# Gate and up products of two token tiles by Strassen's seven block products, in a PE-filled fp4 feed-forward kernel

## The reference

```python
def fp4_linear(x, w):                       # both sides quantized and dequantized in blocks of 16
    return jnp.einsum('bsk,nk->bsn', fp4_quant_dequant(x), fp4_quant_dequant(w))
x = x + tanh(g_xattn) * attention(ctx, ctx, layernorm(x))          # 512 wide, 77 keys a batch
gate = fp4_linear(layernorm(x), w_gate)     # 4096 x 512 by 512 x 1408
y    = fp4_linear(layernorm(x), w_up)       # the same shape
x = x + tanh(g_ffn) * fp4_linear(silu(gate) * y, w_down)           # 4096 x 1408 by 1408 x 512
```

## Time and profile before

| | us |
|---|---|
| time, median of 3 runs (lowest, highest) | 833.9 (832.92, 834.39) |
| span of the profiled execution, first to last instruction | 832.3 |
| TensorE matmul busy in it | 822.4 |
| VectorE busy | 650.7 |
| ScalarE busy | 459.9 |
| GpSimd busy | 400.5 |
| granted TensorE clock, mean | 1.000 |

### The profile page before, as it was taken

How to read it: one execution, slowest core, us unless ns; L and a number is a source line. 1 busy time by engine, 2 the same in 40 slices (tenths; PEclk the granted TensorE clock), 3 DMA queues, 4 the chain that set the end, 5 groups by cost and what they waited for, 6 DMA issues and landing times.

```text
span 832.3 us, 11653 instructions
## 1 busy us (share of the span) xinstructions
PE 822.4 (99%) x4102; PEld 417.0 (50%) x4102; DVE 650.7 (78%) x967; ACT 459.9 (55%) x930; POOL 400.5 (48%) x333
## 2 busy tenths in 40 slices
PE   9999999999999999999999999999999999999998
PEld 5555445444554445444544454445544454444445
DVE  5887899898998698877878688778876878776654
ACT  2778675547555666456563755366646565344320
POOL 3498797764334353444333543454444533444421
PEclk9999999999999999999999999999999999999999
DMA  9723703553243434532641255224433443222232
GB/s 318 285 70 103 157 13 97 122 128 92 48 80 106 108 82 89 129 56 54 114 120 40 55 110 136 61 60 99 97 61 61 85 85 73 58 54 55 48 75 73
DMA packets 192817, 78.21 MB, mean 94 GB/s; under 512 B 176387, under 2 KB 178037, under 8 KB 192759
## 3 DMA queue, kind: packets, MB, share of 16 engines
q1 hardware_dynamic: 192759, 77.47, 39.6%
HBM read 22.76 MB, written 8.39 MB: 37 GB/s over the span
## 4 chain that ended last, share of the span: by engine, by line
PE 93%; ACT 3%; DVE 2%; issue 1%; DMA 1%; POOL 1%; POOLq 0%; ACTq 0%; DVEq 0%
PE banks L1918 60%; PE banks L2037 27%; DVE banks L1417 1%; PE banks L2053 1%; PE banks L1912 1%; PE banks L1971 1%; PE banks L1999 1%; PE banks L1998 1%; PE banks L2143 1%; DMA x_T<-x_parts 1%; PE banks L2150 0%; PE banks L2008 0%; PE banks L2160 0%; PE banks L2165 0%; PE banks L2155 0%
## 5 line engine op out<-in xcount | busy, mean ns | idle before, releaser
L1918 PE MATMUL banks<-wgu_hi,x_T 128*128 128x512 f16 (+1 forms) x1536 | 439.3, 361 | 1.6 <-DMA x_T<-x_parts 0.9
L1918 PE MATMUL banks<-wgu_lo,x_T 128*128 128x512 f16 (+1 forms) x768 | 277.5, 361 | 0.0
L1918 PEld LDWEIGHTS banks<-wgu_hi,x_T 128*128 128x128 f16 x1536 | 150.3, 98 | 155.6 <-issue 1.3
L2037 PE MATMUL banks<-wd,arena 128*128 128x512 f16 x1023 | 227.2, 379 | 0.0
L2037 PEld LDWEIGHTS banks<-wd,arena 128*128 128x128 f16 x1023 | 99.7, 98 | 117.4 <-issue 0.6
L648 POOL TENSOR_TENSOR arena<-arena,h_r 128x1024 f32<-128x1024 f32 (+1 forms) x60 | 93.2, 1554 | 115.3 <-DVE h_r L1372 115.3
L648 POOL TENSOR_TENSOR arena<-arena,h_s 128x1024 f32<-128x1024 f32 x64 | 90.7, 1418 | 88.6 <-DVE arena L1419 53.6
L1918 PEld LDWEIGHTS banks<-wgu_lo,x_T 128*128 128x128 f16 x768 | 75.1, 98 | 76.8 <-issue 0.3
L648 POOL TENSOR_TENSOR xwork<-xwork,x_s 128x512 f32<-128x512 f32 x32 | 38.4, 1201 | 152.0 <-DVE xwork L1419 152.0
L1052 ACT ACTIVATE arena<-banks,scal 128x512 f32<-128x512 f32 (+1 forms) x96 | 61.9, 647 | 84.9 <-PE banks L1918 84.8
L1571 DVE SCALAR_TENSOR_TENSOR arena<-arena,scal,banks 128x512 f32<-128x512 f32 (+1 forms) x90 | 62.2, 694 | 56.3 <-PE banks L1918 53.5
(11 more groups left out here) (199 smaller groups left out, 1043.6 us busy)
## 6 DMA issues: line engine op xcount, KB each, us to landing
ring<-in_x_dram SPq DMA_DIRECT2D x8, 1024.0 KB, 5.1
out_dram<-ring SPq DMA_DIRECT2D x31, 256.0 KB, 2.2
arena<-in_L_ffn_w_down_dram SPq DMA_DIRECT2D x4, 704.0 KB, 5.0
arena<-in_L_ffn_w_gate_dram SPq DMA_DIRECT2D x5, 512.0 KB, 9.7
arena<-in_L_ffn_w_up_dram SPq DMA_DIRECT2D x5, 512.0 KB, 9.6
ring<-in_L_xattn_Wk_dram SPq DMA_DIRECT2D x4, 256.0 KB, 6.1
ring<-in_L_xattn_Wq_dram SPq DMA_DIRECT2D x4, 256.0 KB, 6.8
wd<-in_ctx_dram SPq DMA_DIRECT2D x1, 1024.0 KB
```

The source lines that it names most:

```text
L1918: ended = e.matmul(at, l, r, start=(i == 0), stop=(i == len(terms) - 1))
L2037: ended = e.matmul(by_k(down_ps(t)[:, :], KD), l, r, start=(k == 0 and i == 0), stop=(k == KH - 1 and i == 2))
```

## The change

Tiles 8 to 29 are taken in 11 pairs (a, a + 1). For chunk 0 alone, the gate and up products of both tiles are one 2 by 2 block product: the rows are the two tiles, the inner blocks the two halves of the 512 inputs, the columns the gate and the up weights. Where the kernel before does eight block products (each two k slices, three matmuls each, 512 columns), the new one does seven, in Winograd's form of Strassen's scheme: `pair_product(a, name)` for P1, P5, P6, P2, P7, P3, P4 in this order. The left-hand sums are made from the quantized x on GpSimd (`sum_x`), cast by ScalarE (`sum_high`), their rest by GpSimd (`sum_low`) and transposed by a DMA through `x_parts` (`sum_turn`): two more passes through that buffer a pair. The four sums of weights T1 to T4, 128 x 1024 each, are made once, amid tiles 4 to 7: on GpSimd three instructions for T3 and T1 and two for T2 and T4 (`sum_weights`) and one each for the rest (`low_weights`), on ScalarE a cast each (`high_weights`). Partial results are passed between banks: `copy_p1` and `copy_u3` copy a bank to a bank, `copy_p5` a bank to SBUF, `add_v` and `add_c22` add on VectorE, and `pair_silu`, `pair_hidden` take the place of silu and the multiply for chunk 0.

For these tiles the hidden parts are 512 columns (chunk 0, the last one ready) and 896 columns (chunks 1 and 2), each with a transpose of its own (`part_turn`), and the down product begins with the groups of chunks 1 and 2. Odd tiles use buffers of their own for the parts and scales. x has a ring of 3 slots, the fourth holds weight sums. All five engines have a new order from the first instruction to the last, written out for tiles 0 to 7 and 28 to 31, and as a loop over four tiles (two pairs) between them.

Of the pieces below, `sum_turn` is SP's, `sum_x` and `sum_low` GpSimd's, the copies ScalarE's, the adds VectorE's; after TensorE's loop the last two pieces are VectorE's and ScalarE's lists for the second pair of the loop.

```diff
-    SLOTS = 4
+    SLOTS = 3
+    FIRST_PAIR, PAST_PAIRS = 8, 30
+        STEPS_OF_PAIR = ("P1", "P5", "P6", "P2", "P7", "P3", "P4")
+        BANK_A, BANK_B, BANK_C, BANK_D, BANK_F = 1, 0, 2, 5, 3
+        SUM_ORDER = ("T3", "T2", "T4", "T1")
...
+            def sum_turn(a, i):
+                w.wait_ge(x_lo, place_of_sum(a, i) + 1)
+                if a > FIRST_PAIR:
+                    w.wait_ge(pair_mm, pair_step(a - 2, "P3" if i else "P7"))
...
+                e.dma_start_transpose(sum_T[i], x_parts[:, :]).then_inc(x_turned, 16)
...
+            def sum_x(a):
+                w.wait_ge(x_lo, place_of_x(a + 1) + 1)
+                near, far = slice(0, D // 2), slice(D // 2, D)
+                e.tensor_tensor(x_q2[:, far], x_q2[:, near], x_q2[:, far], ALU.add).then_inc(*step())
+                e.tensor_tensor(x_q2[:, near], x_q[:, near], x_q2[:, near], ALU.subtract).then_inc(x_summed, 1)
...
+                e.tensor_tensor(x_q[:, near], x_q2[:, far], x_q[:, near], ALU.subtract).then_inc(*step())
...
+                e.tensor_tensor(x_q[:, far], x_q[:, far], x_q[:, near], ALU.subtract).then_inc(x_summed, 1)
+            def sum_low(a, i):
+                e.tensor_tensor(x_parts[:, D:2 * D], (x_q2, x_q)[i], x_parts[:, 0:D], ALU.subtract).then_inc(x_lo, 1)
+            def copy_p1(a):
+                w.wait_ge(pair_mm, pair_step(a, "P1"))
+                w.wait_ge(silu_done, SILU(a + 1, 1))
+                e.copy(bank[BANK_B][:, :], bank[BANK_A][:, :]).then_inc(pair_copied, 1)
+            def copy_p5(a):
...
+                e.copy(p5_sb, bank[BANK_F][:, :]).then_inc(pair_copied, 1)
+            def copy_u3(a):
+                w.wait_ge(pair_mm, pair_step(a, "P7"))
...
+                e.copy(bank[BANK_D][:, :], bank[BANK_B][:, :]).then_inc(pair_copied, 1)
...
+            def add_v(a):
+                w.wait_ge(pair_mm, pair_step(a, "P6"))
+                w.wait_ge(h_made, SILU(a + 1, 1))
+                w.wait_ge(*copied(a, "P5"))
+                e.tensor_tensor(bank[BANK_C][:, :], bank[BANK_B][:, :], p5_sb, ALU.add).then_inc(pair_added, 1)
+            def add_c22(a):
...
+                e.tensor_tensor(h_of(b)[:, 0:BANK], bank[BANK_B][:, :], p5_sb, ALU.add).then_inc(pair_added, 1)
...
+            def pair_product(a, name):
+                tokens, ks, weights, at, opens = {
+                    "P1": (of_a, near, quads["B11"], BANK_A, True),
+                    "P2": (of_a, far, quads["B21"], BANK_A, False),
+                    "P3": (of_v[1], far, quads["B22"], BANK_C, False),
+                    "P4": (of_b, far, sums["T4"], BANK_D, False),
+                    "P5": (of_v[0], far, sums["T1"], BANK_F, True),
+                    "P6": (of_v[1], near, sums["T2"], BANK_B, False),
+                    "P7": (of_v[0], near, sums["T3"], BANK_B, False)}[name]
...
+                elif name == "P6":
+                    frees[BANK_B] = added(a, "C22")
+                    w.wait_ge(*copied(a, "P1"))
+                    w.wait_ge(x_turned, 16 * (place_of_sum(a, 1) + 1))
+                elif name == "P7":
+                    w.wait_ge(*added(a, "V"))
+                elif name == "P4":
+                    frees[BANK_D] = (silu_done, SILU(a + 1, 0))
+                    w.wait_ge(*copied(a, "U3"))
...
+                for k in range(2):
+                    for i, (l, r) in enumerate([(hi[:, k, :], weights[0][:, :, k, :]), (hi[:, k, :], weights[1][:, :, k, :]), (lo[:, k, :], weights[0][:, :, k, :])]):
+                        ended = e.matmul(by_k(bank[at][:, :], 4), l, r, start=(opens and k == 0 and i == 0), stop=(k == 1 and i == 2), skip_group_check=True)
...
-            for t in range(7, NT):
+            for t in range(FIRST_PAIR, PAST_PAIRS - 2, TILES):
+                n = t // TILES + 1
+                gate_up(t, 1, 0)
+                gate_up(t, 2, 0)
+                gate_up(t, 1, 1)
+                gate_up(t, 2, 1)
+                down(t - 2, 0)
...
+                gate_up(t + 3, 1, 0)
+                gate_up(t + 3, 2, 0)
+                gate_up(t + 3, 1, 1)
+                pair_product(t + 2, "P1")
+                gate_up(t + 3, 2, 1)
+                down(t + 1, 0)
+                pair_product(t + 2, "P5")
+                pair_product(t + 2, "P6")
+                pair_product(t + 2, "P2")
+                pair_product(t + 2, "P7")
+                att_values(n, 3)
+                pair_product(t + 2, "P3")
+                down(t + 1, 1)
+                pair_product(t + 2, "P4")
+                down(t + 1, 2)
...
+                hidden(t + 3, 2)
+                h_scales(t + 3, 1)
+                h_low(t + 2, 1)
+                x_low(t + 4)
+                add_v(t + 2)
+                h_round(t + 3, 1)
+                values(n, 3)
+                pair_hidden(t + 2, 0)
+                h_scales(t + 2, 0)
+                add_c22(t + 2)
...
+                gate_silu(t + 3, 2)
+                x_squares(t + 4)
+                sum_high(t + 2, 1)
+                if n + 1 < NBATCH:
+                    ln1_sums(n + 1)
+                h_high(t + 2, 1)
+                copy_p1(t + 2)
+                x_high(t + 4)
+                copy_p5(t + 2)
+                h_squares(t + 3, 1)
+                pair_silu(t + 2, 0)
+                if n + 1 < NBATCH:
+                    ln1_squares(n + 1)
+                copy_u3(t + 2)
```

More of the change, by code:

```diff
@@ L208, in build, with x_whole @@
         xT = [[x_T[i][:, p * KD:(p + 1) * KD, :] for p in range(2)] for i in range(2)]
+        sum_T = [valo[:, i, :].bitcast(F16).rearrange("p (k n) -> p k n", k=2 * KD) for i in range(2)]
+        def x_whole(t):
+            return x_q2 if t >= FIRST_PAIR and t % 2 else x_q
         x_parts = sb("x_parts", [P, 2 * D], F16)
@@ L610, in sync_program @@
             x_turn(5)
+            store(0)
             h_turn(3)
@@ new lines, in pool_program @@
+            h_divide(26, 0)
+            h_divide(27, 0)
+            h_times(26, 0)
+            x_times(29)
+            x_stats(30)
+            sum_x(28)
+            h_divide(28, 1)
+            sum_low(28, 0)
+            h_times(27, 0)
+            sum_low(28, 1)
+            x_times(30)
+            h_times(28, 1)
+            x_stats(31)
+            h_divide(29, 1)
+            h_times(29, 1)
+            h_divide(28, 0)
+            h_divide(29, 0)
+            h_times(28, 0)
+            h_times(29, 0)
@@ L835, in scalar_program @@
+            x_times(31)
+            h_divide(30, 0)
+            h_divide(30, 1)
+            h_times(30, 0)
+            h_times(30, 1)
+            h_divide(31, 0)
+            h_divide(31, 1)
+            h_times(31, 0)
+            h_times(31, 1)
         @block.scalar
@@ L1888, in vector_program @@
-            h_round(NT - 1, 1)
-            finish(NT - 3)
-            h_low(NT - 1, 0)
-            h_low(NT - 1, 1)
-            finish(NT - 2)
+            x_divide(8)
+            hidden(7, 0)
+            hidden(7, 1)
+            x_round(8)
+            h_scales(7, 0)
+            x_low(8)
+            key_low(1)
+            finish(4)
+            key_low(2)
+            h_low(6, 1)
+            hidden(7, 2)
+            h_low(6, 0)
+            h_scales(7, 1)
+            h_round(7, 0)
@@ new lines, in vector_program @@
+            h_round(26, 0)
+            finish(25)
+            h_round(27, 0)
+            x_scales(29)
+            x_divide(29)
+            h_low(26, 0)
+            x_round(29)
+            x_low(29)
+            hidden(28, 1)
+            hidden(28, 2)
+            h_scales(28, 1)
+            h_round(28, 1)
+            x_scales(30)
+            hidden(29, 1)
+            finish(26)
+            x_divide(30)
+            hidden(29, 2)
+            x_round(30)
+            h_low(27, 0)
+            h_scales(29, 1)
@@ new lines, in vector_program @@
+            add_v(28)
+            h_low(28, 1)
+            x_low(30)
+            h_round(29, 1)
+            pair_hidden(28, 0)
+            add_c22(28)
+            h_scales(28, 0)
+            finish(27)
+            pair_hidden(28, 1)
+            h_scales(29, 0)
+            h_round(28, 0)
+            h_round(29, 0)
+            x_scales(31)
+            h_low(28, 0)
+            x_divide(31)
+            x_round(31)
+            hidden(30, 0)
+            x_low(31)
+            hidden(30, 1)
@@ new lines, in vector_program @@
+            h_scales(30, 0)
+            hidden(30, 2)
+            h_scales(30, 1)
+            h_round(30, 0)
+            h_low(29, 1)
+            h_low(29, 0)
+            finish(28)
+            h_round(30, 1)
+            hidden(31, 0)
+            hidden(31, 1)
+            h_scales(31, 0)
+            h_low(30, 0)
+            hidden(31, 2)
+            h_scales(31, 1)
+            h_round(31, 0)
+            h_low(30, 1)
+            h_round(31, 1)
+            finish(29)
+            h_low(31, 0)
@@ new lines, in tensor_program @@
+            gate_up(28, 1, 1)
+            down(26, 1)
```

(31 more changed lines are left out.)

1527 lines of the change are left out of this document (912 added, 615 removed).

## The result

The changed kernel takes 853.36 us (median of 4 runs, 851.88 to 854.21), beside 833.41 for the kernel before on the same chip (832.34 to 834.39): ratio 1.0237, interval 1.0221 to 1.0253. It is slower by 20 us, where 12 us less were forecast. The profiled execution has a span of 852.4 us, and the forecast's span was 819.8: 32.6 us are to be found.

A forecast was written before the change was run, and what follows sets the result against it. TensorE, without gaps in the loop, was taken as the bound: 832.3 - 14.2 + 1.0 + 1.2 + 0.5 - 1.0 = 819.8 us of span, median 1.6 above, 821.4. The likeliest case's range was 818 to 824.5, the overall range 816.5 to 829.

The forecast's parts named there:

- 66 matmuls at 0.216: -14.2.: TensorE, chunk 0 of gate and up: six fewer matmuls a pair in 11 pairs, at 0.216 us each: -14.2 us.
- I take +0.5: Ahead of tile 8: fourteen GpSimd instructions for weight sums, 32 us, may hold VectorE: +0.5 us, bounds 0 and 8.
- The new order ... -1.0: Ahead of tile 8: value_product(4) fills places where TensorE had waited 0.7 and 0.9 us: -1.0 us, bounds -4 and +4.
- The first half of h ... slack 1.4; I take 0.: Loop, chunk 0 of h before down's last group: 18 us on four queues against about 19.4, cost 0.
- The average therefore costs nothing: Loop: no engine off the path exceeds 86.3 us in four tiles, VectorE at about 73, so cost 0.
- an operation is held on average for less than half of the other's length: Loop, argument against VectorE becoming the bound: holds by GpSimd's operations last, on average, under half the other's length.
- +8.8: GpSimd, four tiles of the loop: eight half-width operations and four sum_low add 8.8 us, to 49.
- `add_v` +1.0: Loop, between P6 and P7: VectorE's add has slack of about 1; 0.1 us a pair, 1.0 in all, bounds 0 and 1.3.
- the copy of U3 +1.2: Loop, P4 waits for ScalarE's copy, late by 0.3 us in four second pairs: +1.2 us, bounds 0 and 0.9 a pair.
- The rival that named VectorE: Loop: added GpSimd operations hold VectorE, which becomes the bound at 91.4 us a period: +14, 848 us, chance 0.07.

The follow-up runs named there:

- all_q: Changed kernel, GpSimd's weight and activation sums and down weights' multiplications cut to few columns, h_low(t, 0) moved up, store(t-1) put behind the part's transpose: 822.32 us, ratio 0.9873.
- x_small: Changed kernel, with the six GpSimd instructions a pair that make the sums of x cut to 8 columns each: 848.31 us, ratio 1.0190.
- both_small: Changed kernel, with GpSimd's sums of x cut to 8 columns and almost no sums of weights: 836.35 us, ratio 1.0038.

## Why the prediction was wrong

By its own steps.

- **"66 matmuls at 0.216: -14.2."** Right. With the rest out of the way, `all_q` has a span of 820.5, where the forecast had 819.8, and its four tiles take 86.9 to 87.2 us where I had named 86.3 to 87. The gain exists; the changed kernel spends it. That the two spans lie so near each other is in part chance: `all_q` also lacks the down weights' multiplications, which the forecast had left in.
- **"I take +0.5" for the sums of weights.** The step that failed worst: 10.5 us (12.0 once the activations' sums are cut). My own bound was 8. The two waits for `finish` and the stretches behind them hold most of it. I had the very hold in the earlier trace rows and priced it by room on average, "both queues have room". VectorE had 155.59 of 179.47 in that stage, no room at 87%, and a hold of 2 us ahead of a `finish` or a `hidden` becomes a wait, and then a stretch at half clock behind it.
- **"The new order ... -1.0" for the start.** With GpSimd's work cut it is about that: `all_q` has 1287 matmuls in its first 285.00 us, the kernel before 1284 in 285.15. But at 125 us four GpSimd multiplications in a row hold VectorE 6 us. Cutting them gave 8.9 us, a part of which the kernel before might have had as well: it has these instructions too, and waits of 1.6 us there. I looked only at where TensorE had waited, not at what else the reorder put side by side. (I also passed over its second longest wait, 1.2 us for ScalarE at 38 us.)
- **"The first half of h ... slack 1.4; I take 0."** I walked four engines' queues and used a transpose's usual landing, but not SyncE's: `store` waits for its landing and loads 1 MB ahead of the transpose. 4.9 us, by the move of that one call. In the changed kernel it is a wait each period, 1.1 to 1.5 us, the first 2.4 with a half-clock stretch.
- **"The average therefore costs nothing"**, with VectorE at 73 of 86.3 us: it has 81.4 in 88.75. The count of instructions was right, their lengths were not. Of the 8 us above it, the added sums explain 2 (`x_small`); even in `both_small` it is 80 of 89.5. The rest comes from old instructions that now meet. Yet `all_q` keeps the forecast's period with 81.5 of 89.5: what failed is less the average than the walk through the hand-overs, which used the lengths of the old trace. VectorE's groups, 454.69 to 543.44 us of the changed kernel:

```profile
L2000 DVE TENSOR_TENSOR arena<-arena 128x896 f16<-128x896 f32 x3 | 6.2, 2058 | 0.0
L1789 DVE SCALAR_TENSOR_TENSOR arena<-arena 128x512 f32<-128x512 bf16 x4 | 5.6, 1406 | 0.1
...
L1924 DVE TENSOR_TENSOR x_parts<-xwork,x_parts 128x512 f16<-128x512 f32 x2 | 3.8, 1900 | 0.0
...
L2000 DVE TENSOR_TENSOR h_parts<-arena,h_parts 128x896 f16<-128x896 f32 x2 | 2.1, 1052 | 0.0
```

  The same 896 columns take 1.05 us at one place of the order and 2.06 at the other; `x_low` takes 1.90 for one tile in two and 0.71 for the other. In the kernel before it took 0.63 in every tile of the loop. In the changed one 15 of the loop's 20 `x_low` end 0.55 us behind an instruction of line 790 (`h_divide` or `h_times`, both old) that had begun ahead of them. I had argued that "an operation is held on average for less than half of the other's length", but an order that repeats every four tiles has no average: one `x_low` of each period, at 382.9, 471.8, 560.5 and 651.3 us, takes 2.20 us each time. In `both_small`, without the added sums, the meeting is still there:

```profile
456.64 2.43 POOL L790 TENSOR_TENSOR arena<-arena 128x896 f32<-128x896 f32 x1 [3.49 <-DVE arena L1742]
457.42 2.20 DVE L1924 TENSOR_TENSOR x_parts<-xwork,x_parts 128x512 f16<-128x512 f32 x1
```

- **GpSimd "+8.8".** 14.1 us by the groups of that stretch, since these instructions grow as well: 256 columns took 0.73 to 1.34 us for my 0.55, 512 columns 1.27 to 1.81 for 1.1. Cost of the sums of activations: 5.1 to 6.5 us, priced at 0.
- **`add_v` +1.0 and the copy of U3 +1.2.** P7's waits for `add_v` are 1.6 us in all, about as taken. P4 has no wait for the copy of U3 in the rows; that term was 0.
- **The rival that named VectorE** (848, chance 0.07) had the right engine and the right sign, and it is luck that its time is near: it put all of the loss into the loop, from the sums of activations, which cost 5 to 6.5 of the 32 us, and the stage ahead of tile 8 lost 12.3. It also needed VectorE to fill the period, and `all_q` shows TensorE nearly without gaps beside a VectorE as busy as that.

The ledger, each figure the difference of two medians: 853.4, less 10.5 (sums of weights), 6.5 (sums of activations), 0.2 (`h_low` up), 8.9 (down weights' multiplications), 4.9 (store behind the transpose) = 822.3; forecast 821.4. The medians come from several chips, on which the kernel before took 832.5 to 833.4 us, and part of each term is the number of half-clock stretches, so a term is good to about 1 us and the 0.2 is nothing. The terms are not independent: the first two are worth 1.5 us more together than one by one. Three of the five were had by leaving work out, so 822.3 is no kernel. The fastest whole version of the change, 848.5, stays behind the kernel before.

Left open: how the cost of GpSimd's sums divides into holds of VectorE and its own lateness, outside the places shown; and whether an order exists that keeps the old multiplications apart from VectorE's two-input instructions.

## What to carry to other kernels

An engine off the path has to be counted with the lengths that its instructions have beside their new neighbours, not with those of the old trace: 22 us of holds spread over the kernel before cost nothing, and 2.8 us of them ahead of one `finish` cost a wait and a half-clock stretch. Where a hold falls decides, more than how busy the engine is. An order that repeats meets the same neighbour each time, so a hold there is not to be averaged. Walk every queue in front of a hand-over, the DMA-issuing one too, with what each of its entries itself waits for. And when the chain names one late link, look for a second behind it before moving the first: `h_low` moved alone gave 0, moving the store gave 5.

## What the runs showed of the hardware

- In the changed kernel's trace six waits of TensorE of 1.8 to 4.1 us each had about 3.4 us at a granted clock near 0.5 (the 1.2 GHz level) behind them, and four of 1.1 to 1.5 us had none; a wait of 3.1 us thus cost up to 4.8. It is no rule: `x_small` waited 3.2 us at 309 us and 2.0 at 319 with a granted clock of 1.00 behind both, and round its wait of 4.1 us the clock was at 0.50 for 6.8 us.
- A `tensor_scalar` of 128x64, usually 0.25 us, took 2.05 us beside a 2.14 us GpSimd instruction; GpSimd's own 256 column operations took 0.73 us at one place of the order and 1.34 at another. Both engines' instructions lengthen.
- `x_low`, 0.63 us alone, ended 0.55 us behind the GpSimd instruction beside it, whatever was left of that: 0.72 to 2.20 us in all. That fits an instruction that waits for the end and then runs.
- A transpose of 8 blocks issued beside a load of 1 MB landed after 6.04 us; the transposes of x, 8 blocks too, take 3.2 as a rule.
